# Running maximum over the feed-forward channels: halving of pieces replaced by a chain of joins, with new orders on all engines

## The chip, the cores and the metric

The kernel runs on 1 core of one Trainium2 chip. The metric is the time of one execution on the device in microseconds (us), and less is better. An execution under the hardware profiler gives the trace; its time and its span (first to last instruction) are told apart below.

## The reference

Sixteen images are cut into 36 patches each, projected to 256 channels, joined with a class token and 128 text tokens (165 tokens per sample), and sent through one transformer block: windowed attention, then a feed-forward part whose inputs and weights are rounded to a few levels.

```python
h = tok(x, W_lin, b_lin, class_token, position_embeddings)   # (16, 37, 256)
h = concatenate([h, txt], axis=1)                            # (16, 165, 256)
h = h + attn(layernorm(h))       # 16 heads, 4 KV heads, rotary, keys within 32 positions
h = h + ffn(layernorm(h))

def act_quant(x):
    scale = 127.0 / clip(max(abs(x), axis=-1, keepdims=True), 1e-05)
    return clip(round(x * scale), -128, 127) / scale

def ffn(x):
    h = einsum('bsd,hd->bsh', act_quant(x), weight_quant(w1))   # 256 -> 1024 channels
    h = depthwise_conv1d(h, conv_w, conv_b)                     # 3 taps along the tokens
    h = silu(h)
    return einsum('bsh,dh->bsd', act_quant(h), weight_quant(w2))
```

The part that the change rewrites is `max(abs(x), axis=-1)` of the second `act_quant`: for each token the largest magnitude over 1024 channels.

## The kernel before

**Tiling.** Two samples make a pair: 330 tokens, 3 token tiles (t) of 110. There are 8 pairs (n = 0 to 7). Attention goes over 11 blocks (j) of 30 queries with up to 94 keys. The feed-forward part has the 1024 channels in 8 tiles (m) of 128 partitions, each with 330 columns.

**The steps that the prediction names.** At the head: `sort_pix`, `turn_pix` and `keep_pix` reorder image rows, `patch` (L1636, L1638) projects a group of tokens, `keep_patch` copies it out, and SyncE's `move_tokens` moves it to `h` by DMA. `stats1_of` (L1337 to L1344) is the first layer norm's statistics; it waits for the tokens of its pair. `project` (L1689) makes queries, keys and values; `rope_first` (L1363 to L1378) or GpSimd's `rope` rotates them; `turn_q` (L1702) and `turn_k` (L1718) turn them; `keep_k_first` (L1384) copies keys out of PSUM. For each block `scores` (L1741 to L1752), `max_s` (L1393, VectorE), `shift` (L1760), `exp` (L1145), `turn_p` (L1769), `keep_p` (L1154) and `context` (L1784) follow one another. `abs_w` (L1307) sums the magnitudes of the feed-forward weights.

In the feed-forward part of a pair, `up` (L1840, L1841) fills a bank, ScalarE's `mid` (L1190) and VectorE's `taps` (L1449, L1452) do the convolution into `u`, `tanh` (L1198) with `silu` (L1458 on VectorE, L1043 and L1045 on GpSimd) gives the activation in place, and ScalarE's `abs_g` (L1206) writes magnitudes of a piece into the tile `ga`. A piece is 4 channel tiles (2 pieces a pair), and 2 channel tiles in the last pair (4 pieces).

**The maximum.** For pairs 0 to 6, `max_g` halves each piece: 4 tiles to 2 (L1475, 660 columns), 2 to 1 (L1479, 330 columns), and after the second piece joins the two results (L1482, 330 columns). In the last pair each piece of 2 tiles goes to 1 (L1468) and, from the second piece on, is joined to the result (L1473). The result is in `gm`. `turn_max` (L1849) turns it, `scale_2` (L1489 to L1495) makes the scale, `spread` (L1855) lays it over 128 partitions, `quant_g` (L1502) or `quant_last` (L1553) scales the activation to int8, `conv_g` (L1213) or `conv_last` (L1233) makes it bf16, `down` (L1867) multiplies, and `add_ffn` (L1510) adds to `h`. All pieces share `ga`, so `abs_g` of a piece waits (semaphore `part_maxed`) until the piece before it has been reduced.

**The last pair's input.** Its second layer norm goes tile by tile on VectorE: `var_last` (L1516, L1518), GpSimd's `rstd_last` (L1049), `norm_last` (seven instructions, L1523 to L1540), `turn_last` (L1874), ScalarE's `high_last` (L1227) and VectorE's `low_last` (L1546).

**What sets the order.** Every engine runs its own instructions in order. Each step has a place number per engine in the table `ORDER` (or `ONCE`), written out by hand; each engine walks the numbers upward and issues what is due. Semaphores alone tie the engines together. GpSimd and SyncE have such tables as well.

## Time and profile before

| | |
|---|---|
| median of 3 runs | 401.66 us (400.25 to 404.05) |
| the profiled execution | 399.73 us |
| its span | 397.9 us |
| mean granted TensorE clock | 0.956 |
| TensorE busy | 343.9 us (86%) |
| VectorE busy | 302.5 us (76%) |
| ScalarE busy | 259.2 us (65%) |
| GpSimd busy | 248.2 us (62%) |

PE is the matmul engine (TensorE), PEld its weight loads, DVE is VectorE, ACT is ScalarE, POOL is GpSimd and SP is SyncE. Busy time is an average over stages that are bound by different things, so it is read stage by stage. A matmul's record can overlap the next one's, because they are pipelined.

### The profile page before, as it was taken

How to read it: one execution, taken by the hardware profiler on the slowest of the kernel's cores; microseconds unless marked ns; L12 is line 12 of the kernel's file. 1: busy time of each engine (PE TensorE's matmuls, PEld its weight loads, DVE VectorE, ACT ScalarE, POOL GpSimd, SP SyncE). 2: the span in 40 equal slices, each digit the busy share in tenths (PEclk: the TensorE clock that was granted, in tenths of full speed). 3: DMA queues.
4: the chain of work that ended last, by engine and by line, in shares of the span. 5: the costliest groups of instructions: out<-in, count | busy, mean ns of one | idle time of the engine just before them, and what ended most of it. 6: DMA issues, size and time to landing. Idle time of an engine off the chain costs nothing.

```text
span 397.9 us, 8286 instructions
## 1 busy us (share of the span) xinstructions
PE 343.9 (86%) x2910; PEld 267.9 (67%) x2910; DVE 302.5 (76%) x643; ACT 259.2 (65%) x486; POOL 248.2 (62%) x244
## 2 busy tenths in 40 slices
PE   1579999999999989999999997989989989844564
PEld 1356666767787668867986796778857857634454
DVE  2164548744568889897889759998888899898984
ACT  3232554857767869867887767679777787534732
POOL 3407189299899994999489957991760563051510
PEclk9998999999999999999999999999999999995856
DMA  7772161000000100020001002000010210001001
GB/s 233 170 163 55 34 213 28 16 13 15 26 20 18 35 1 3 17 59 20 6 18 33 9 18 61 17 0 2 2 26 22 69 49 1 2 0 36 1 16 52
DMA packets 20250, 15.71 MB, mean 39 GB/s; under 512 B 11035, under 2 KB 19160, under 8 KB 20209
## 3 DMA queue, kind: packets, MB, share of 16 engines
q1 hardware_dynamic: 19314, 14.02, 13.7%
q10 hardware_dynamic: 895, 1.16, 1.1%
q8 instruction: 23, 0.38, 0.4%
q14 instruction: 18, 0.15, 0.1%
HBM read 7.91 MB, written 2.70 MB: 27 GB/s over the span
## 4 chain that ended last, share of the span: by engine, by line
PE 49%; DVE 20%; POOL 14%; issue 6%; DMA 5%; ACT 4%; SPq 1%; ACTq 0%; DVEq 0%; POOLq 0%
PE bank L1769 6%; PE bank L1840 4%; PE bank L1867 4%; PE bank L1784 3%; PE bank L1841 3%; POOL shared L1027 3%; PE bank L1741 3%; PE bank L1689 3%; PE bank L1760 3%; PE bank L1811 3%; DMA cst<-in_consts 3%; PE bank L1636 2%; POOL shared L1035 2%; PE bank L1752 2%; PE bank L1802 2%
## 5 line engine op out<-in xcount | busy, mean ns | idle before, releaser
L1393 DVE TENSOR_REDUCE mx<-bank 120x4 fp32r<-120x376 f32 (+3 forms) x88 | 44.5, 509 | 29.7 <-PE bank L1752 28.9
L1154 ACT COPY pT<-bank 94x480 f32<-94x480 f32 (+3 forms) x88 | 48.6, 555 | 15.4 <-PE bank L1769 14.9
L1145 ACT ACTIVATE pr<-bank 120x376 f32<-120x376 f32 (+3 forms) x88 | 39.9, 457 | 26.0 <-PE bank L1760 25.2
L1769 PE MATMUL bank<-cst,pr 120*94 120x120 f32 (+3 forms) x352 | 51.1, 269 | 3.2 <-ACT pr L1145 2.8
L1840 PE MATMUL bank<-xT_hi,w1T 128*128 128x330 f32 x128 | 45.6, 362 | 4.1 <-DVE wn L1452 2.4
L1769 PEld LDWEIGHTS bank<-cst,pr 120*94 120x94 f32 (+3 forms) x352 | 36.6, 121 | 12.5 <-ACT pr L1145 6.7
L1841 PE MATMUL bank<-xT_lo,w1T 128*128 128x330 f32 x128 | 41.1, 326 | 0.0
L1689 PE MATMUL bank<-wqk,xnT 128*110 128x384 f32 x96 | 36.8, 512 | 0.2
L1760 PE MATMUL bank<-mx,neg_id 120*120 120x376 f32 (+3 forms) x88 | 33.0, 386 | 4.0 <-DVE mx L1393 3.9
L1867 PE MATMUL bank<-w2T,shared 128*110 128x256 bf16 x192 | 29.2, 305 | 8.0 <-DVE h L1510 3.7
L1752 PE MATMUL bank<-kbd,q_hl 128*120 128x376 f32 (+3 forms) x88 | 36.1, 410 | 0.0
L1741 PE MATMUL bank<-kbd,q_hl 128*120 128x376 f32 (+3 forms) x88 | 35.6, 405 | 0.5 <-ACT pT L1154 0.4
L1043 POOL TENSOR_TENSOR shared<-shared,wn 128x1320 f32<-128x1320 f32 (+1 forms) x5 | 12.2, 2436 | 35.0 <-ACT shared L1198 35.0
L983 POOL TENSOR_SCALAR xn<-h,mv,rs 110x256 f32<-110x256 f32 x21 | 27.9, 1336 | 9.6 <-PE bank L1677 9.4
L1784 PE MATMUL bank<-pT,vw 94*32 94x120 f32 (+3 forms) x704 | 33.5, 286 | 0.2
L1867 PEld LDWEIGHTS bank<-w2T,shared 128*110 128x110 bf16 x192 | 24.6, 146 | 10.6 <-issue 5.3
L976 POOL TENSOR_TENSOR rs<-ve,half_neg 110x3 f32<-110x3 f32 x15 | 15.1, 1005 | 25.5 <-DVE ve L1344 18.9
L1027 POOL TENSOR_SCALAR shared<-h,mv,rs 110x256 f32<-110x256 f32 x21 | 30.2, 1449 | 1.1 <-POOL rs L976 1.1
L1840 PEld LDWEIGHTS bank<-xT_hi,w1T 128*128 128x128 f32 x128 | 25.5, 199 | 7.3 <-DVE wn L1452 3.2
L1035 POOL TENSOR_SCALAR shared<-shared,am 110x256 f32<-110x256 f32 x21 | 25.4, 1220 | 6.4 <-ACT shared L1174 6.4
L1005 POOL TENSOR_TENSOR qkr<-rc,rsn 110x160 f32<-110x160 f32 x44 | 26.8, 631 | 1.7
L1784 PEld LDWEIGHTS bank<-pT,vw 94*32 94x32 f32 (+3 forms) x704 | 18.8, 144 | 12.1 <-issue 8.2
(149 smaller groups left out, 918.4 us busy)
## 6 DMA issues: line engine op xcount, KB each, us to landing
out<-h SPq DMA_DIRECT2D x7, 330.0 KB
...
```

What stands on the lines that cost most here:

```text
L1027: o = nc.gpsimd.tensor_scalar(xn2[:, t, :], h[:, n, t, :], mv2[:, t, 0:1], rs2[:, t:t + 1], ALU.subtract, ALU.mult)
L1154: nc.scalar.copy(pT[0:cnt, g % 3, :], S_BANKS[g % 2][0:cnt, 0:HKV * QP]).then_inc(p_kept, 1)
L1393: nc.vector.tensor_reduce(mx[:, g % 4, :].bitcast(F32R), S_BANKS[g % 2][0:QP, 0:HKV * KEYS[j][1]].rearrange("p (k c) -> p k c", k=HKV), ax ...
L1689: o = nc.tensor.matmul(qk_bank(n, t)[0:TT, 0:QKC + QK], xnT[:, k, t * TT:(t + 1) * TT], wqk[:, k, :], start=(k == 0), stop=(k == KD - 1))
L1741: nc.tensor.matmul(dst, q, kbd[n % 2][:, 0, :, k0:k0 + cnt].bitcast(F32R), start=True, stop=False)
L1752: o = nc.tensor.matmul(dst, q, kbd[n % 2][:, 1, :, k0:k0 + cnt].bitcast(F32R), start=False, stop=True)
L1760: nc.tensor.matmul(S_BANKS[g % 2][0:QP, 0:HKV * cnt], neg_id[:, :].bitcast(F32R), mx[:, g % 4, :].bitcast(F32R).unsqueeze(2).to_broadcast( ...
L1769: o = nc.tensor.transpose(S_BANKS[g % 2][0:cnt, kv * QP:(kv + 1) * QP], pr[:, g % 3, kv * cnt:(kv + 1) * cnt], ident[0:QP, 0:QP])
L1784: o = nc.tensor.matmul(C_BANK[VS * kv:VS * (kv + 1), col:col + QP], vw[n % 2][0:cnt, j, :, kv], pT[0:cnt, g % 3, kv * QP:(kv + 1) * QP], s ...
L1840: nc.tensor.matmul(dst, w, xT_hi[:, k, :].bitcast(F32R), start=(k == 0), stop=False)
L1841: o = nc.tensor.matmul(dst, w, xT_lo[:, k, :].bitcast(F32R), start=False, stop=(k == KD - 1))
L1867: o = nc.tensor.matmul(down_bank(n, t), gq[:, m, t * TT:(t + 1) * TT], w2T[:, m, :], start=(m == 0), stop=(m == MH - 1))
```

## The change

The tile `ga` has 6 channel tiles in place of 4, and `gm` one in place of 3. In pairs 0 to 6 the first piece's magnitudes go to tiles 0 to 3 and the second's to tiles 2 to 5. Tiles 0 and 1 hold the running maximum and take in two more tiles at a time: one join of 660 columns for the first piece, two for the second, and at the end tile 0 with tile 1 into `gm` (330 columns). In the last pair the four pieces go to tiles 0, 2, 4 and 2, with three joins and the same end. Lines of the changed kernel are some 5 to 9 higher: the joins are L1482 there and the end is L1487.

```diff
+def ga_of(n, p):
+    if n < PAIRS - 1:
+        return (slice(0, 4), slice(2, 6))[p]
+    at = (0, 2, 4, 2)[p]
+    return slice(at, at + 2)
...
-        gm, at = carve(shared, at, 128, [3, T])
+        gm, at = carve(shared, at, 128, [T])
...
-        ga, at = carve(shared, at, 128, [HALFC, T])
+        ga, at = carve(shared, at, 128, [6, T])
...
             def abs_g(n, p):
-                at = NP * n + p
-                act.wait_ge(silued, at + 1)
-                if at:
-                    act.wait_ge(part_maxed, at)
                 ms = gate(n, p)
-                nc.scalar.activation(ga[:, 0:ms.stop - ms.start, :], u_of(n)[:, ms, :], ACT.Abs).then_inc(g_absed, 1)
+                act.wait_ge(silued, NP * n + p + 1)
+                if n and p == 0:
+                    act.wait_ge(g_maxed, n)
+                if p and ga_of(n, p).start == 2 and (n < PAIRS - 1 or p > 1):
+                    act.wait_ge(joined, 3 * n + 1)
+                nc.scalar.activation(ga[:, ga_of(n, p), :], u_of(n)[:, ms, :], ACT.Abs).then_inc(g_absed, 1)
...
             def max_g(n, p):
...
+                    joins = ((), (2,), (4,), (2,))[p]
+                    first = 3 * n + p
+                else:
+                    joins = ((2,), (2, 4))[p]
+                    first = 3 * n + p + 1
+                if joins:
+                    dve.wait_ge(g_absed, NP * n + p + 1)
+                for i, at in enumerate(joins):
+                    if first + i > 3 * n + 1:
+                        dve.wait_ge(joined, first + i - 1)
+                    nc.vector.tensor_tensor(ga[:, 0:2, :], ga[:, 0:2, :], ga[:, at:at + 2, :], ALU.max).then_inc(joined, 1)
+                if gate(n, p).stop == MH:
+                    dve.wait_ge(joined, 3 * (n + 1))
+                    if n:
                         dve.wait_ge(max_turned, n)
...
+                    nc.vector.tensor_tensor(gm[:, :], ga[:, 0, :], ga[:, 1, :], ALU.max).then_inc(g_maxed, 1)
...
             def turn_max(n):
-                pe.wait_ge(g_maxed, n + (1 if n < PAIRS - 1 else 3))
+                pe.wait_ge(g_maxed, n + 1)
```

Nearly all rows of `ORDER` and `ONCE` change too, on all engines. Two of them:

```diff
-    'pe.patches': (1, 9, 10, 16),
+    'pe.patches': (1, 8, 11, 12),
...
-    'dve.norm_last': (284, 293, 300),
+    'dve.norm_last': (281, 298, 299),
```

**TensorE at the head**, from the first `turn_q` (L1702 before, L1707 now) to the first `scores` (L1741 before, L1746 now). L1636 and L1638 (now L1641 and L1643) are `patch`, L1718 (now L1723) is `turn_k`. Before:

```order
L1689 MATMUL bank<-wqk,xnT 110x384 x6
L1636 MATMUL bank<-wlT,wn 126x256 x6
L1638 MATMUL bank<-posb,cst 126x256
L1636 MATMUL bank<-wlT,wn 126x256 x6
L1638 MATMUL bank<-posb,cst 126x256
L1702 MATMUL bank<-cst,qsp 128x110 x8
L1718 MATMUL bank<-cst,qsp 128x110 x6
L1702 MATMUL bank<-cst,qsp 128x110 x4
L1636 MATMUL bank<-wlT,wn 126x256 x6
L1638 MATMUL bank<-posb,cst 126x256
L1741 MATMUL bank<-kbd,q_hl 120x264
```

Now:

```order
L1694 MATMUL bank<-wqk,xnT 110x384 x2
L1707 MATMUL bank<-cst,qsp 128x110 x4
L1641 MATMUL bank<-wlT,wn 126x256 x6
L1643 MATMUL bank<-posb,cst 126x256
L1641 MATMUL bank<-wlT,wn 126x256 x6
L1643 MATMUL bank<-posb,cst 126x256
L1707 MATMUL bank<-cst,qsp 128x110 x4
L1723 MATMUL bank<-cst,qsp 128x110 x6
L1707 MATMUL bank<-cst,qsp 128x110 x4
L1682 MATMUL bank<-cst,xn 128x110 x3
L1746 MATMUL bank<-kbd,q_hl 120x264
```

The last `patch` stood between `turn_k` and the first `scores`; now it stands ahead of `turn_k`, and 3 transposes of the next pair's `xn` stand in its place.

**VectorE at the head**, from the copy of the first pair's keys (L1384 before, L1393 now) on. L1337 to L1344 (now L1346 to L1353) are `stats1_of`, L1393 (now L1402) is `max_s`, L1307 (now L1316) is `abs_w`. Before:

```order
L1384 TENSOR_SCALAR kbd<-bank,cst 128x330 x4
L1393 TENSOR_REDUCE mx<-bank 120x4 x2
L1337 BN_STATS st<-h 110x6 x3
L1341 BN_AGGR mv<-st 110x2 x3
L1344 TENSOR_SCALAR ve<-mv 110x3
L1393 TENSOR_REDUCE mx<-bank 120x4 x4
L1307 TENSOR_REDUCE wabs<-wn 128x1
L1393 TENSOR_REDUCE mx<-bank 120x4
```

Now:

```order
L1393 TENSOR_SCALAR kbd<-bank,cst 128x330 x4
L1346 BN_STATS st<-h 110x6 x3
L1350 BN_AGGR mv<-st 110x2 x3
L1353 TENSOR_SCALAR ve<-mv 110x3
L1402 TENSOR_REDUCE mx<-bank 120x4 x2
L1346 BN_STATS st<-h 110x6 x3
L1350 BN_AGGR mv<-st 110x2 x3
L1353 TENSOR_SCALAR ve<-mv 110x3
L1402 TENSOR_REDUCE mx<-bank 120x4 x2
L1316 TENSOR_REDUCE wabs<-wn 128x1 x2
L1402 TENSOR_REDUCE mx<-bank 120x4 x2
```

The statistics of pair 2 stood behind the first two maxima and now stand ahead of them; the two sums over weights stand together, ahead of the fifth maximum.

**VectorE at the end of pair 6**, around the last pair's input. L1523 (now L1528) begins `norm_last` and L1540 (now L1545) ends it, L1458 of 1320 columns (now L1467) is `silu`, L1475 to L1482 (now L1482 and L1487) are `max_g`, L1546 (now L1551) is `low_last`. Before:

```order
L1523 TENSOR_SCALAR shared<-h,mv,rs 110x256
...
L1540 TENSOR_SCALAR shared<-shared,am 110x256
L1449 SCALAR_TENSOR_TENSOR shared<-bank,conv,shared 128x2x164
...
L1458 SCALAR_TENSOR_TENSOR shared<-shared 128x1320
L1523 TENSOR_SCALAR shared<-h,mv,rs 110x256
...
L1475 TENSOR_TENSOR shared<-shared 128x660
L1479 TENSOR_TENSOR shared<-shared 128x330
L1546 TENSOR_TENSOR xT_lo<-bank,xT_hi 128x2x220
```

Now:

```order
L1461 SCALAR_TENSOR_TENSOR shared<-bank,conv,shared 128x2x164
L1521 BN_AGGR mv<-st 110x2
L1523 TENSOR_SCALAR ve<-mv 110x1
L1528 TENSOR_SCALAR shared<-h,mv,rs 110x256
...
L1545 TENSOR_SCALAR shared<-shared,am 110x256
L1528 TENSOR_SCALAR shared<-h,mv,rs 110x256
...
L1482 TENSOR_TENSOR shared<-shared 128x660
L1467 SCALAR_TENSOR_TENSOR shared<-shared 128x1320
L1551 TENSOR_TENSOR xT_lo<-bank,xT_hi 128x2x220
```

`norm_last` of tile 1 stood with two channel tiles of `taps` behind it; now both `norm_last` steps stand together behind all `taps` of the pair, and `silu` stands behind them.

## Rows read from the trace of the kernel before

**Rows 1.** Busy time by stretch, each engine in turn, granted clock, DMA share, GB/s

```profile
40.00:60.00 20.00, 19.06 (x131) 13.42 (x131) 10.40 (x24) 10.91 (x25) 10.54 (x14) 1.00 0.37 123
...
80.00:100.00 20.00, 19.65 (x184) 14.53 (x183) 9.04 (x27) 12.71 (x26) 19.09 (x24) 1.00 0.06 14
...
160.00:180.00 20.00, 19.26 (x170) 14.53 (x169) 18.89 (x42) 14.87 (x29) 19.38 (x16) 1.00 0.15 38
...
360.00:380.00 20.00, 11.65 (x48) 9.88 (x48) 18.49 (x38) 11.62 (x16) 6.36 (x4) 0.67 0.02 8
```

**Rows 2.** The chain that ended last, shares of the span by engine

```profile
PE 49%; DVE 20%; POOL 14%; issue 6%; DMA 5%; ACT 4%; SPq 1%; ACTq 0%; DVEq 0%; POOLq 0%
```

**Rows 3.** TensorE in order of time, 27 to 48 us

```profile
27.64 0.94 PE L1623 MATMUL bank<-cst,shared 72*128 72x72 f32 x12 [0.16 <-DVE wn L1298]
...
40.74 0.98 PE L1702 MATMUL bank<-cst,qsp 110*128 110x110 f32 x8
41.91 0.76 PE L1718 MATMUL bank<-cst,qsp 110*128 110x110 f32 x6 [0.19 <-DVE qsp L1378]
...
42.87 2.77 PE L1636 MATMUL bank<-wlT,wn 128*126 128x256 f32 x12
...
46.20 0.39 PE L1741 MATMUL bank<-kbd,q_hl 128*120 128x264 f32 x1
...
47.35 0.37 PE L1760 MATMUL bank<-mx,neg_id 120*120 120x264 f32 x1
```

**Rows 4.** VectorE in order of time, 42 to 58 us

```profile
42.70 1.97 DVE L1384 TENSOR_SCALAR kbd<-bank,cst 128x330 fp32r<-128x330 f32 x4 [0.94 <-PE bank L1718]
...
46.87 1.00 DVE L1393 TENSOR_REDUCE mx<-bank 120x4 fp32r<-120x264 f32 x2 [2.20 <-PE bank L1752]
...
49.20 1.08 DVE L1337 BATCH_NORM_STATS2 st<-h 110x6 f32<-110x256 f32 x3 [1.33 <-DMA h<-tokp]
...
50.66 0.17 DVE L1344 TENSOR_SCALAR ve<-mv 110x3 f32<-110x3 f32 x1
...
57.81 2.28 DVE L1307 TENSOR_REDUCE wabs<-wn 128x1 f32<-128x2048 f32 x1
```

**Rows 5.** SyncE's queue in order of time, 31 to 48 us

```profile
31.53 13.09 SPq L922 DMA_DIRECT2D vw<-qk  x17
44.66 3.03 SPq L900 DMA_DIRECT2D h<-tokp  x4
```

**Rows 6.** VectorE by line: instructions of the maximum, busy us and mean ns

```profile
L1475 DVE TENSOR_TENSOR shared<-shared 128x660 f32<-128x660 f32 x14 | 13.3, 952 | 1.1 <-ACT shared L1206 0.8
...
L1479 DVE TENSOR_TENSOR shared<-shared 128x330 f32<-128x330 f32 x14 | 10.9, 777 | 0.5
...
L1482 DVE TENSOR_TENSOR shared<-shared 128x330 f32<-128x330 f32 x7 | 4.9, 699 | 0.2
```

**Rows 7.** The wide ones: duration in ns min/median/max

```profile
L1475 DVE TENSOR_TENSOR shared<-shared x14: 836/848/1577, 133.4 to 364.8; 128x660 f32<-128x660 f32 x14
```

**Rows 8.** VectorE in order of time, 342 to 360 us

```profile
342.81 0.35 DVE L1537 TENSOR_SCALAR shared<-shared,am 110x256 f32<-110x256 f32 x1
...
345.51 0.56 DVE L1452 SCALAR_TENSOR_TENSOR shared<-bank,conv,shared 128x328 f32<-128x328 f32 x1
...
349.89 1.16 DVE L1523 TENSOR_SCALAR shared<-h,mv,rs 110x256 f32<-110x256 f32 x1
...
352.04 2.05 DVE L1537 TENSOR_SCALAR shared<-shared,am 110x256 f32<-110x256 f32 x1
...
359.95 0.41 DVE L1523 TENSOR_SCALAR shared<-h,mv,rs 110x256 f32<-110x256 f32 x1 [0.44 <-POOL rs L1049]
```

**Rows 9.** GpSimd in order of time, 347 to 354 us

```profile
347.88 3.02 POOL L1043 TENSOR_TENSOR shared<-shared 128x1320 f32<-128x1320 f32 x1
350.97 2.97 POOL L1045 TENSOR_TENSOR shared<-shared 128x1320 f32<-128x1320 f32 x1
```

**Rows 10.** VectorE in order of time, at 384 us

```profile
384.56 0.50 DVE L1468 TENSOR_TENSOR shared<-shared 128x330 f32<-128x330 f32 x1 [0.34 <-ACT shared L1206]
```

More of the change, by code:

```diff
@@ L147 @@
+        (24, 28, 39),
+        (86, 90, 96),
+        (136, 141, 144),
+        (191, 195, 202),
+        (253, 264, 277),
+        (338, 343, 348),
+        (405, 415, 420),
     ),
     'pe.turn_q': (
-        (11, 12, 15),
-        (46, 57, 66),
-        (105, 116, 121),
-        (154, 169, 174),
-        (208, 225, 230),
-        (287, 300, 312),
-        (360, 371, 384),
-        (447, 452, 460),
+        (10, 13, 16),
+        (43, 47, 57),
+        (101, 113, 121),
+        (153, 169, 172),
@@ L157 @@
+        (206, 224, 232),
+        (289, 298, 318),
+        (352, 367, 385),
+        (438, 453, 460),
     ),
     'pe.turn_k': (
-        (13, 14),
-        (68, 73),
-        (124, None),
-        (179, None),
-        (239, None),
-        (322, None),
-        (387, None),
-        (485, None),
+        (14, 15),
+        (64, 71),
+        (125, None),
+        (176, None),
+        (237, None),
+        (324, None),
+        (393, None),
+        (495, None),
     ),
     'pe.scores': (
[8 rows of a table removed]
[8 rows of a table added]
@@ L262 @@
-        (533, 542, 554),
-        (581, 592, 601),
+        (234, 242, 257),
+        (304, 314, 332),
+        (382, 398, 425),
+        (470, 482, 490),
+        (528, 536, 561),
+        (590, 596, 599),
         (616, 617, 618),
@@ L333 @@
-        (283, 305, 318),
-        (340, 352, 366),
-        (384, 402, 414),
+        (31, 46, 58),
+        (75, 92, 104),
+        (125, 146, 162),
+        (189, 198, 217),
+        (237, 253, 264),
+        (284, 303, 322),
+        (340, 352, 369),
+        (385, 398, 412),
     ),
     'act.keep_sel': (
-        (39, 51, 64),
-        (83, 97, 111),
-        (135, 154, 169),
-        (193, 205, 226),
+        (39, 51, 65),
+        (84, 101, 113),
+        (138, 155, 171),
+        (195, 206, 226),
@@ L447 @@
         (31, None),
-        (40, None),
+        (39, None),
         (50, None),
```

369 lines of the change are left out of this document (167 added, 202 removed), and 160 rows, old and new, of the table ORDER.

## The prediction

> **What bounds the kernel now.** I read the table of busy time by stretch first, since whole-span shares mix stages [rows 1]. The reader is to see three regimes. Up to about 150 us TensorE is nearly always busy (19.65 of 20 us at 80 to 100 us) and GpSimd too (19.09), while VectorE has half its time free (9.04). From 160 us on VectorE is nearly as full as TensorE (18.89 and 19.26). After 360 us VectorE alone is full (18.49) and TensorE is at 11.65. The chain of work that ended last says the same: TensorE 49%, VectorE 20%, GpSimd 14% [rows 2]. So time taken from VectorE is worth nothing early, something in the middle, and all of it at the end; and a delay of TensorE at the head is not easily won back.
>
> The profiled execution took 399.73 us with a span of 397.9; the median of the runs is 401.66, that is 1.93 above it. I make the sum as a difference to the profiled execution and put it on the median.
>
> **The joins.** Per pair (0 to 6) before: two instructions of 660 columns and three of 330. After: three of 660 and one of 330. The columns are equal (2310); one instruction fewer is issued and two narrow ones become one wide. By the means of the trace before [rows 6]: 2 x 0.952 + 2 x 0.777 + 0.699 = 4.157 us; after: 3 x 0.952 + 0.699 = 3.555 us; 0.60 less. By the shortest wide one [rows 7] and a narrow one of 0.50 [rows 10]: 2 x 0.836 + 3 x 0.50 = 3.17 and 3 x 0.836 + 0.50 = 3.01; 0.16 less. The two differ because narrow instructions ran much longer than 0.50 us on average (0.777, 0.699), and wide ones up to 1.577: each seems to pay for something on top of its columns, so fewer instructions pay less often. I take 0.4 a pair, between the two. It counts where VectorE is last to come: pairs 2 to 6, five pairs, 2.0 us. Pairs 0 and 1 fall before or about 160 us, where VectorE has room. Bounds: 5 x 0.16 = 0.8 and 7 x 0.60 = 4.2. Term: **-2.0** (0.8 to 4.2 less). The new waits (`joined`) stand on instructions that were in a chain before too, and the second piece's magnitudes now wait for one instruction, not two.
>
> There is a rule that speaks against wide joins. The long ones have a partner: a VectorE instruction of 0.35 us took 2.05 us while GpSimd ran one of 2.97, and it ended 0.15 us behind that one's end (352.04 + 2.05 = 354.09, and 350.97 + 2.97 = 353.94) [rows 8, 9]. The Trainium skill, "SBUF — State Buffer" (the part on the port pair that VectorE and GpSimd share), says that the pair is an exclusive lock held for a whole instruction, and counts a VectorE instruction with two SBUF inputs among those that contend. By that rule GpSimd in turn waits for a join up to 0.85 us where it waited up to 0.50, and pair 0's three joins lie in GpSimd's full stretch: 3 x 0.35 = 1.05 us later there, and the whole sum would be -1.7 where it is -2.7 without. The trace bears out the lock, but shows no GpSimd instruction that waits for a join alone, so I leave it out of the sum and inside the range.
>
> **The head.** Two moves work together, and both go against the kernel. First, TensorE. Before, `turn_k` began at 41.91, the copy of the keys ran from 42.70 to 44.67 while the last `patch` ran (42.87 to 46.20), and `scores` began at 46.20 with no wait [rows 3, 4]. Now that `patch` stands ahead of `turn_k`. What comes before it is otherwise the same work, less the turns that move behind (one of the two `turn_q` that began at 40.74, and all up to 42.87: about 1.6 us) and plus one `turn_pix` (0.94 us) that began at 27.64, when the engine had idle time, and now stands behind the first `project`; the patches end near 46.20 - 1.6 + 0.95 = 45.5, `turn_k` begins near 46.0, the key copy starts 0.8 later and ends near 48.8. `scores` start there, 2.6 us later, and only a short transpose fills the gap. Second, VectorE. `stats1_of` of pair 2 now stands ahead of the first `max_s`. It waits for tokens that landed at 49.20, and they cannot come sooner: SyncE issues them at 44.66 to 47.69, behind 17 transfers that it issues from 31.53 without a break [rows 4, 5], and SyncE's order up to there is unchanged. The statistics end at 50.66 + 0.17 = 50.83, and the first `max_s` starts there and not at 46.87: **4.0 us later**. `shift` follows it as before (47.35). In that time TensorE does about 0.5 us of work that came later before, so it is 3.5 us behind.
>
> How much of that is still there at the end? TensorE in 40 to 60 us was busy 19.06 of 20 [rows 1], so there is 0.9 us per 20 to win back, about 1.3 up to 80 us by this and a little more by the weights, whose second sum now stands beside the first and not apart. I take **+2.2**. Bounds: 0 (all of it hidden later) and +3.9, and with the two sums over weights together ahead of the fifth `max_s` (2.28 us more in one piece [rows 4]) up to +6.2.
>
> **The end of pair 6.** Before, `norm_last` of tile 1 met GpSimd's `silu`. Its first instruction took 1.16 us and its sixth 2.05, where the first took 0.41 for tile 2 and the sixth 0.35 for tile 0 [rows 8]; each ended just after a GpSimd instruction of 3 us ended (350.90 and 353.94) [rows 9]. That is 0.75 + 1.70 = 2.45 us, on an engine that is full there, and 0.44 us of idle time before tile 2's step comes on top: 2.9. In the new order `norm_last` of tiles 1 and 2 stand behind all eight `taps`. GpSimd's `silu` started 1.8 us after the fourth channel tile's taps ended (346.07 to 347.88) and lasted 6.1, till +7.9; VectorE has about 7.3 us of other work up to `norm_last` (four more channel tiles at 2 x 0.56, two `add_ffn`, one attention add with its statistics, one normalization of the context). So it gets there near the end of `silu`, and one small instruction (`ve`, 0.17 us) may wait up to 0.8. Term: -2.9 + 0.8 = **-2.1**, bounds 0 (another instruction waits in place of these) and -2.9. What is late next: `low_last` then follows `silu` on VectorE, which covers the way over TensorE and ScalarE.
>
> **The last pair.** Four instructions (3 x 0.85 + 0.50 = 3.05) for seven (7 x 0.50 = 3.5) [rows 7, 10]: 0.45 less, on the path, since VectorE is full here. The idle gap of 0.34 ahead of the last piece [rows 10] should close: `tanh` of the first piece stands earlier, and the last piece's magnitudes go to other tiles than the piece before and need no longer wait for it. Against it: behind the last magnitudes there are now 0.85 + 0.50 us and not 0.50 + 0.50. Term: **-0.8**, bounds 0 and -1.1. From `gm` to the end nothing changes.
>
> **The middle.** All rows move by a few places. The number of matmuls is the same, and counting what stands ahead of each pair's steps gives shifts of either sign of about 1 us. I cost it at 0, with 2.5 us to either side from the size of one such stall in the rows (2.05) [rows 8].
>
> **The sum.** -2.0 + 2.2 - 2.1 - 0.8 + 0 = -2.7 us. The profiled execution would be 397.0 us, the median 401.66 - 2.7 = **399.0 us**.
>
> **Rivals.**
> 1. *The head decides.* First `max_s` 4 us late, then the two weight sums in one piece hold `max_s` back again: +6.2, against gains of 2.0 + 2.1 + 0.8 = 4.9. That gives +1.3, 403.0 us, slower than before. It decides from a head loss of 4.9 us on. For it speaks that TensorE and GpSimd have under 1 us of slack in 20 at 80 to 100 us; against it that VectorE has half its time free there, so that what comes late to it does not queue as well.
> 2. *VectorE's relief counts everywhere.* Joins at the mean, all seven pairs (-4.2), head mostly hidden (+0.5), the end as forecast (-2.1 - 0.8): -6.6, 395.1 us. For it: VectorE's 18.89 of 20 at 160 us; against: TensorE's 19.26 there [rows 1].
> 3. *The end's waits only move.* The lock takes as much in another place (0 for the end of pair 6), joins hidden (-0.8), head +1.5, last pair -0.5: +0.2, 401.9 us. For it: contention goes by chance of place, and the new order was not the only thing that kept these apart. This is also the case in which the change of the maximum does not do what it says.
>
> **Chances.** Forecast (397.5 to 401) 0.39; rival 1 and what lies above 402.5 0.16; rival 2 and what lies below 397.5 0.28; rival 3 0.17. The range reaches from rival 2 to a little past rival 1, so that about 0.1 is left out at either end: 395.0 to 403.8. About 1% (4 us) is what a measurement of this kernel can tell from no change. Faster by over 1% means under 397.6: rival 2's 0.28 and the lowest 0.03 of the forecast, 0.31. Slower by over 1% means over 405.7, which is rival 1 with the middle's 2.5 us against it as well (405.5) and beyond: 0.10. Between: 0.59.
>
> **What would show it.** Head: VectorE's first TENSOR_REDUCE of `mx` near 50.8 and first `scores` near 48.8; if the maximum comes near 47, the head step is wrong. Statistics of pair 2 waiting for the DMA till 49.2 just ahead of it. TensorE's busy time in 40 to 60 us falls by some 2 us. Joins of pairs 0 to 6: the wide ones near 0.95 on average, and with the last narrow ones some 25 us in sum, not 13.3 + 10.9 + 4.9 = 29.1 [rows 6]. End of pair 6: both `norm_last` steps about 2.1 us each with no instruction over 1 us. Last pair: no idle time ahead of its last joins. The prediction fails if the middle moves by more than 2.5 us: then one of the new places puts a step of VectorE or GpSimd behind a wait that nobody needs.

## The result

The changed kernel is slower: the median of four runs is 407.12 us (405.46 to 409.70), of the kernel before beside it 402.86 us, ratio 1.014 with a 95% interval of 1.008 to 1.020. Medians are over all runs, while every ratio here and below leaves out runs in the chip's slower state, among them one of 407.82 us of the kernel before, whose other three have the median of 401.66 that the prediction started from. The forecast was 399.0 us, 2.7 less than 401.66; measured are 5.5 more. The profiled execution took 405.46 us with a span of 403.4, against 399.73 and 397.9. The table by stretch, columns as in [rows 1]:

```profile
40.00:60.00 20.00, 16.68 (x89) 11.07 (x87) 10.89 (x29) 7.67 (x19) 10.27 (x13) 0.83 0.38 127
80.00:100.00 20.00, 19.75 (x179) 14.97 (x176) 10.33 (x28) 15.02 (x30) 15.64 (x21) 1.00 0.05 11
160.00:180.00 20.00, 18.34 (x153) 14.11 (x150) 17.01 (x34) 15.48 (x29) 17.02 (x10) 1.00 0.15 37
360.00:380.00 20.00, 10.03 (x40) 8.15 (x39) 18.33 (x41) 11.01 (x15) 6.29 (x4) 0.64 0.02 6
```

From 40 to 60 us TensorE is busy 16.68 us in place of 19.06, issues 89 instructions in place of 131, and its granted clock is 0.83 and no longer 1.00. The chain that ended last, by engine (against [rows 2]), has more TensorE, less VectorE, and SyncE's queue in it:

```profile
PE 65%; DVE 10%; SPq 7%; ACT 6%; issue 4%; POOL 4%; DMA 3%; ACTq 0%; DVEq 0%; POOLq 0%
```

TensorE in order of time, 44 to 58 us, where [rows 3] went from the turn of the keys through the last patch into the scores:

```profile
44.08 0.73 PE L1723 MATMUL bank<-cst,qsp 110*128 110x110 f32 x6
...
47.04 0.47 PE L1682 MATMUL bank<-cst,xn 110*128 110x110 f32 x3 [1.85 <-ACT q_hl L1131]
47.37 0.36 PE L1746 MATMUL bank<-kbd,q_hl 128*120 128x264 f32 x1
...
50.23 1.11 PE L1765 MATMUL bank<-mx,neg_id 120*120 120x264 f32 x2 [0.80 <-DVE mx L1402]
...
52.09 2.77 PE L1694 MATMUL bank<-wqk,xnT 128*110 128x384 f32 x4
...
55.25 0.41 PE L1746 MATMUL bank<-kbd,q_hl 128*120 128x376 f32 x1
```

VectorE in order of time, 44 to 62 us (against [rows 4]):

```profile
44.84 1.97 DVE L1393 TENSOR_SCALAR kbd<-bank,cst 128x330 fp32r<-128x330 f32 x4 [3.33 <-PE bank L1723]
48.21 1.08 DVE L1346 BATCH_NORM_STATS2 st<-h 110x6 f32<-110x256 f32 x3 [1.40 <-DMA h<-tokp]
...
49.75 0.87 DVE L1402 TENSOR_REDUCE mx<-bank 120x4 fp32r<-120x264 f32 x2
54.76 1.08 DVE L1346 BATCH_NORM_STATS2 st<-h 110x6 f32<-110x256 f32 x3 [4.13 <-POOL xn L991]
...
57.34 4.47 DVE L1316 TENSOR_REDUCE wabs<-wn 128x1 f32<-128x2048 f32 x2
```

The first `scores` began at 47.37 and not 46.20, the first `max_s` at 49.75 and not 46.87, both with a wait ahead of them: TensorE's 1.85 us are for ScalarE's copy of the turned queries (L1131), VectorE's 1.40 us for the tokens of pair 2. A second wait of 4.13 us stands on the statistics of pair 3, which are held by GpSimd's norm of pair 2. The projection of four matmuls at 52.09 took 2.77 us, at half the clock (1.54 us before). The granted clock (last but two column) in steps of 4 us, 46 to 58 us:

```profile
46.00:50.00 4.00, 2.33 (x12) 1.64 (x12) 2.53 (x10) 1.65 (x5) 0.07 (x1) 0.79 0.48 144
50.00:54.00 4.00, 3.77 (x9) 2.23 (x10) 0.63 (x2) 1.92 (x5) 3.82 (x4) 0.50 1.02 377
54.00:58.00 4.00, 3.81 (x17) 2.44 (x16) 3.13 (x10) 1.03 (x2) 3.09 (x5) 0.85 0.22 66
```

0.50 is the 1.2 GHz level. The clock fell between 48 and 49 us, behind the wait of 1.85 us and ahead of the one of 0.80. Against full speed the 12 us lack 4 x (0.21 + 0.50 + 0.15) = 3.4 us of clock, idle time included.

I followed one mark through both traces: the start of TensorE's `turn_xn` of pair n. Pair 2's came 3.6 us later than before (76.9), pair 3's 4.0 (101.5), pair 5's 3.8 (163.0), pair 6's 4.7 (204.5), and the run ended 5.5 later. Pair 1's scores came 3.3 us later (81.49 and 78.15). So about 4 of the 5.5 us are lost by pair 3's mark, and nothing wins them back. In between it is more for a time: pair 7's mark is 6.8 us late. The maximum itself did what it should; VectorE by line (against [rows 6]):

```profile
L1482 DVE TENSOR_TENSOR shared<-shared 128x660 f32<-128x660 f32 x24 | 22.3, 931 | 0.9 <-ACT shared L1215 0.6
L1487 DVE TENSOR_TENSOR shared<-shared 128x330 f32<-128x330 f32 x8 | 4.8, 604 | 0.3
```

The last pair's four are in it (0.84 + 0.84 + 0.85 + 0.51 = 3.04 us from 386 to 391 us), so those of pairs 0 to 6 take 27.1 - 3.0 = 24.1 us in place of 29.1. At the end of pair 6 `norm_last` of tile 1 runs from 362.40 to 364.55 without a long instruction, for GpSimd's `silu` was over by then (to 362.43):

```profile
362.40 0.41 DVE L1528 TENSOR_SCALAR shared<-h,mv,rs 110x256 f32<-110x256 f32 x1
...
363.81 0.35 DVE L1542 TENSOR_SCALAR shared<-shared,am 110x256 f32<-110x256 f32 x1
```

### The profile page after: what moved, and what is told of

Its sections match the earlier page's. It is cut to its first block, busy times and chain, and to the rows that moved or that the text cites. A ratio compares the mean times of both kernels' runs of the same rounds, so it can differ in the third digit from the quotient of the medians.

```text
span 403.4 us, 8281 instructions
## 1 busy us (share of the span) xinstructions
PE 351.0 (87%) x2910; PEld 272.4 (68%) x2910; DVE 295.3 (73%) x633; ACT 260.7 (65%) x486; POOL 244.8 (61%) x244
## 4 chain that ended last, share of the span: by engine, by line
PE 65%; DVE 10%; SPq 7%; ACT 6%; issue 4%; POOL 4%; DMA 3%; ACTq 0%; DVEq 0%; POOLq 0%
PE bank L1774 8%; PE bank L1694 7%; PE bank L1789 6%; SPq L930 6%; PE bank L1816 5%; PE bank L1845 5%; PE bank L1872 4%; PE bank L1746 4%; PE bank L1846 4%; PE bank L1765 4%; PE bank L1807 3%; PE bank L1757 3%; PE bank L1641 2%; DMA cst<-in_consts 2%; DVE shared L1482 2%
## 5 line engine op out<-in xcount | busy, mean ns | idle before, releaser
L1402 DVE TENSOR_REDUCE mx<-bank 120x4 fp32r<-120x376 f32 (+3 forms) x88 | 44.7, 511 | 35.5 <-PE bank L1757 35.0
L1845 PE MATMUL bank<-xT_hi,w1T 128*128 128x330 f32 x128 | 46.6, 368 | 5.5 <-DVE wn L1461 2.8
L1846 PE MATMUL bank<-xT_lo,w1T 128*128 128x330 f32 x128 | 42.3, 335 | 0.0
L1746 PE MATMUL bank<-kbd,q_hl 128*120 128x376 f32 (+3 forms) x88 | 35.9, 408 | 4.1 <-ACT pT L1162 3.8
L1765 PE MATMUL bank<-mx,neg_id 120*120 120x376 f32 (+3 forms) x88 | 35.7, 409 | 2.4 <-DVE mx L1402 1.9
L991 POOL TENSOR_SCALAR xn<-h,mv,rs 110x256 f32<-110x256 f32 x21 | 26.0, 1248 | 12.9 <-PE bank L1682 12.5
L1845 PEld LDWEIGHTS bank<-xT_hi,w1T 128*128 128x128 f32 x128 | 26.3, 206 | 8.7 <-DVE wn L1461 4.0
L1035 POOL TENSOR_SCALAR shared<-h,mv,rs 110x256 f32<-110x256 f32 x21 | 29.3, 1404 | 1.2 <-POOL rs L984 1.1
L1872 PEld LDWEIGHTS bank<-w2T,shared 128*110 128x110 bf16 x192 | 25.5, 149 | 5.3 <-ACT shared L1242 2.5
L1013 POOL TENSOR_TENSOR qkr<-rc,rsn 110x160 f32<-110x160 f32 x44 | 27.8, 654 | 1.7
L1198 ACT ACTIVATE shared<-bank,conv 128x330 f32<-128x330 f32 x32 | 20.0, 627 | 12.6 <-PE bank L1846 11.7
```

The lines of the kernel that those rows point to most:

```text
L1402: nc.vector.tensor_reduce(mx[:, g % 4, :].bitcast(F32R), S_BANKS[g % 2][0:QP, 0:HKV * KEYS[j][1]].rearrange("p (k c) -> p k c", k=HKV), ax ...
L1746: nc.tensor.matmul(dst, q, kbd[n % 2][:, 0, :, k0:k0 + cnt].bitcast(F32R), start=True, stop=False)
L1765: nc.tensor.matmul(S_BANKS[g % 2][0:QP, 0:HKV * cnt], neg_id[:, :].bitcast(F32R), mx[:, g % 4, :].bitcast(F32R).unsqueeze(2).to_broadcast( ...
L1845: nc.tensor.matmul(dst, w, xT_hi[:, k, :].bitcast(F32R), start=(k == 0), stop=False)
L1846: o = nc.tensor.matmul(dst, w, xT_lo[:, k, :].bitcast(F32R), start=False, stop=(k == KD - 1))
L1872: o = nc.tensor.matmul(down_bank(n, t), gq[:, m, t * TT:(t + 1) * TT], w2T[:, m, :], start=(m == 0), stop=(m == MH - 1))
```

## The experiments

Each kernel was timed in five rounds beside the kernel before, and those of a group on the same chip (`e18` and `e19` on another than the rest of their group). In the tables of places a number is only a rank, so an edit is shown as the move that it makes.

**First group: which part?** The places up to the start of the third pair ("the head") and the rest were crossed.

`e1`: the chain in the code, all old places.

> The chain of joins in the code, all tables of places of the kernel before (piece 0 of the last pair has no join and so no item). Theory T1 (the new order at the head costs about 4 us, the chain itself is worth little): 401.4 to 402.4 where the kernel before shows 402.9, a ratio of 0.996 to 1.000, first max_s(0,0) within 0.5 us of the kernel before. Rival R1 (the chain itself makes the loss: its joins wait on the abs, abs on the join): 405 or more, ratio over 1.005. Rival R2 (the joins are worth the full 2 us of the forecast and only the new order hid it): 400.9 or less, ratio under 0.995.

402.64 us, ratio 0.998 (0.993 to 1.003). As T1 had it. The lower end of the interval is 2.7 us under the kernel before, so it leaves room for R2's 2 us as well.

`e2`: the halving in the code, all new places.

> The halving of pieces as in the kernel before, with the new tables of places (the last pair's piece 0 gets its place back, behind its last taps). T1: the loss of the head is all there, 406.5 to 408.5, ratio 1.009 to 1.014. R1: the loss goes with the chain, 402 to 404, ratio under 1.004. R2: slower than the changed kernel by 2 us, 409, ratio 1.015.

408.55 us, ratio 1.012 (1.006 to 1.019). The loss is there without the chain: R1 is refuted.

`e3` and `e4`: the chain with old head and new rest, and with new head and old rest.

> The chain, and on each engine the items of the old order up to the start of the third pair (TensorE's first 77 items, VectorE's 33, ScalarE's 55, GpSimd's 11, SyncE's 8), then all others in the new order. T1: the 3.5 to 4 us that the traces show by 78 us are gone, 402.4 to 404.0, ratio 0.999 to 1.003. Rival R3 (the middle of the new order loses as much by itself, and would lose it with any head): 406 or more, ratio over 1.008.

> The mirror of the kernel with the old head: the chain, the items of the new order up to the start of the third pair, then all others in the old order. T1: 405.5 to 407, ratio 1.007 to 1.011. R3: 402.5 to 403.5, ratio under 1.003.

401.61 us, 0.998 (0.995 to 1.001), and 408.82 us, 1.015 (1.009 to 1.022). The order at the head is the whole loss: 1.8% or 7 us from `e1` to `e4`, by the intervals some 4 to 10. The new order behind it costs nothing that can be measured. In the trace of `e4` the second pair's scores start 4.5 us later than before, and the mark of pair 3 does too. In `e3` the same stretch has the full clock:

```profile
46.00:50.00 4.00, 3.63 (x24) 2.63 (x22) 0.97 (x2) 1.04 (x3) 0.00 (x0) 1.00 0.15 38
50.00:54.00 4.00, 3.73 (x26) 2.27 (x23) 2.11 (x8) 2.22 (x6) 2.05 (x3) 1.00 0.93 286
```

**Second group: which move of the head, and what is a join worth?** My theory was that the two statistics on VectorE make the loss.

```diff
 dve, e5: changed kernel with
-  stats1(2), max_s(0,0), max_s(0,1), stats1(3), max_s(0,2) ...
+  max_s(0,0), max_s(0,1), stats1(2), max_s(0,2) ... max_s(0,6), stats1(3)
 pool, e5:
-  rope(1,0), rstd1(3), rope(1,1), rope(1,2)
+  rope(1,0), rope(1,1), rope(1,2), rstd1(3)
```

> The changed kernel with the statistics of pair 2 behind max_s(0,1) and those of pair 3 behind max_s(0,6) again, and GpSimd's rstd1 of pair 3 behind rope(1,2), as before; all else new. Theory T1s (the loss at the head is made by the two waits of the statistics on VectorE, for a transfer and for GpSimd's norm, and by the TensorE clock that falls behind them): first max_s near 48, clock 1.00 from 48 to 58, start of the second pair's scores 2.5 to 4 us earlier than in the changed kernel, time 403 to 404.5. Rival T1p (the loss comes from TensorE's own gap of 1.85 us at 45 to 47, where the last patches no longer fill the wait for ScalarE, and the clock falls for that): the clock still falls to 0.5, at least 2 us of the loss stay, 406 or more.

407.86 us, 1.012 (1.007 to 1.016). The clock stays at 1.00 from 46 to 62 us as T1s says, and yet nothing is won. TensorE in order of time, near 67 us:

```profile
62.21 1.33 PE L1907 MATMUL bank<-cst,pr 120*78 120x120 f32 x8
66.83 0.74 PE L1840 MATMUL bank<-cst,qsp 110*128 110x110 f32 x4 [3.30 <-POOL qsp L1160]
```

This is `turn_q(1,1)`, which waits for GpSimd's rope of pair 1. The new order has it ahead of `scores(0,6)`, the old one behind `scores(0,8)`. Behind the wait the clock is 0.65 from 66 to 70 us. Both theories fall: one stall is gone and another has its place.

`e6` puts only the statistics of pair 3 back.

> The changed kernel with only the statistics of pair 3 (and GpSimd's rstd1 of pair 3) back at their old places; those of pair 2 stay ahead of max_s(0,0). If the second wait of 4.1 us on VectorE costs what its place suggests: 404.5 to 405.5, start of the second pair's scores 1.5 to 2.5 us earlier than in the changed kernel. If TensorE at half its clock reaches the third scores only at 55.3 anyway, so that the wait is covered: 406.5 to 407.5, under 0.7 us earlier.

404.95 us, 1.003 (0.999 to 1.008); in the trace, whose execution was the longest of its six (406.82), the wait of 4.1 us is gone and pair 3's mark is at 105.7 us against 105.5 in the changed kernel. The trace is for "covered", the median for the other; I leave it open. The interval lies wholly below that of the changed kernel (1.008 to 1.020), though that was timed in another session, so this one move may hold a good part of the loss.

```diff
 pe, e7: changed kernel with
-  patches 2, patches 3, turn_q(0,1), turn_k(0,0), turn_k(0,1), turn_q(0,2)
+  patches 2, turn_q(0,1), turn_k(0,0), turn_k(0,1), turn_q(0,2), patches 3
```

> The changed kernel with the last patches of TensorE (patches 3) behind turn_q(0,2) again, in the gap of 1.85 us ahead of the second pair's turn_xn; all else new, both statistics ahead as in the change. T1s: TensorE still waits for the first max_s, the clock still falls, 406 to 408. T1p: the gap is filled, the clock stays at 1.00 from 46 to 56, start of the second pair's scores 2 to 3 us earlier, 404 to 405.

405.63 us, 1.006 (1.001 to 1.010), profiled 406.96. The gap of 1.85 us is filled, the first scores start 1.5 us earlier, and TensorE waits for the first maximum instead, with the clock at 0.51 from 50 to 54 us again:

```profile
47.13 0.42 PE L1890 MATMUL bank<-kbd,q_hl 128*120 128x368 f32 x1
50.71 1.11 PE L1898 MATMUL bank<-mx,neg_id 120*120 120x264 f32 x2 [3.15 <-DVE mx L1535]
```

`e10`, on `e1`, does each join twice in pairs 0 to 6:

```diff
+                    if n < PAIRS - 1:
+                        nc.vector.tensor_tensor(ga[:, 0:2, :], ga[:, 0:2, :], ga[:, at:at + 2, :], ALU.max).then_inc(rejoined, 1)
+                        dve.wait_ge(rejoined, first + i)
                     nc.vector.tensor_tensor(ga[:, 0:2, :], ga[:, 0:2, :], ga[:, at:at + 2, :], ALU.max).then_inc(joined, 1)
```

> The chain with the old tables of places, and in pairs 0 to 6 each join of two tiles is done twice (the maximum is not changed by it): 21 more instructions of about 0.93 us, 19.5 us more of VectorE's busy time, 2.8 us per pair. Theory T2 (in the middle TensorE's queue sets the end and the joins lie beside it): 402.5 to 405, so under 2 us for 19.5. Rival (half of the joins' time shows, which is how the prediction came to 2.0 us for 4.1): 412 or more.

428.37 us, 1.063 (1.059 to 1.067). T2 falls: 21 more joins of 0.998 us on average (20.9 us) cost 25.4 us, more than they last. (The rival ascribes to the prediction that half of the joins' time shows; it had counted 0.4 us in each of five pairs in full.) The marks tell where: against the kernel before, pair 4's is 0.3 us late, when no join has run yet, pair 5's 4.0, pair 6's 8.3 and pair 7's 11.5.

**Third group: up and down from the joins, and two more moves.** `e12` cuts the joins of pairs 0 to 6 to 8 columns a tile (`ga[:, 0:2, 0:8]`), `e13` repeats only the last join of a pair.

> The chain with the old tables of places; in pairs 0 to 6 each join of two tiles takes the maximum of 8 columns of each tile alone (the others are left out, so most tokens get a scale from 2 tiles only), 21 instructions of about 0.1 us for 0.93: 17 us less of VectorE's busy time. Theory T4 (what is saved on VectorE is not wanted there: TensorE's queue is 94 to 99 per cent busy in the middle): 401 to 402.5, less than 2 us. Rival (VectorE sets the pace in the middle, as the kernel with each join done twice has it, 25 us for 19.5): 396 or less.

399.82 us, 0.993 (0.990 to 0.996), so 2.9 us less. That lies between the two, nearer to T4. It does not decide R2, since it measures from the chain downwards and not from the halving to the chain. The 21 short joins took 0.31 us each and not 0.1. VectorE by line has all 24 joins at 9.1 us, where `e1` has 23.4:

```profile
L1616 DVE TENSOR_TENSOR shared<-shared 128x16 f32<-128x16 f32 (+1 forms) x24 | 9.1, 379 | 1.6 <-ACT shared L1348 1.0
```

> The chain with the old tables of places, and in pairs 0 to 6 only the last join of a pair is done twice: 7 more instructions of 0.93 us, 6.5 us more of VectorE's time, 0.9 per pair. In proportion to the kernel with 21 more, 25.7 us for 19.5, it would be 411; if there is slack below a step of that size, 403 to 406.

419.21 us, 1.041 (1.036 to 1.047): 16.7 us for 7 instructions of 1.162 us. The trace has a wait of 2.4 us for `qsp` and the clock at 0.65 from 46 to 50 us before there is any join, and its first scores come at 49.88, 3.7 us later than before. Counted from the first scores to the end it is 14.7 us longer than `e1`'s trace. Downwards 14.3 us of joins bring 2.9; upwards 8.1 us cost 15 to 17. TensorE in order of time at 150 us shows how:

```profile
147.83 0.60 PE L1843 MATMUL bank<-cst,qsp 110*128 110x110 f32 x4
150.34 0.54 PE L1990 MATMUL bank<-cst,shared 128*110 128x128 f32 x3 [1.91 <-DVE shared L1623]
...
151.17 0.95 PE L1910 MATMUL bank<-cst,pr 120*94 120x120 f32 x4
```

and by stretch, same kernel:

```profile
145.00:150.00 5.00, 2.96 (x23) 1.65 (x21) 4.77 (x6) 3.23 (x7) 4.92 (x6) 1.00 0.00 0
150.00:155.00 5.00, 4.66 (x25) 4.54 (x26) 3.28 (x11) 1.03 (x2) 4.75 (x7) 0.66 0.00 0
```

`turn_max` stands in TensorE's queue where the maximum has just come; 1.91 us late, TensorE idles, and then works at a lower clock (four transposes 0.95 us, where they took 0.57 at full clock). Against the kernel before, pair 2's scores come 3.8 us late and pair 3's 6.2: 2.4 us for one join more.

`e9` undoes one swap: GpSimd's `norm1(2)` behind `rope(1,0)`.

> The changed kernel with one swap undone: GpSimd's norm1 of pair 2 behind rope(1,0) again instead of ahead of it. The statistics of pair 3 on VectorE still wait for that norm. If the wait on VectorE is what costs (the prediction's way of thinking), it grows from 4.1 us by the rope's 3 to 4 us and all later maxima with it: second pair's scores at 84 or later, 409 or more. If the late rope costs instead (it hands TensorE the second pair's turned queries), the time falls: second pair's scores 1 to 2 us earlier than in the changed kernel, 405 to 406.

416.13 us, 1.032 (1.027 to 1.037). The prediction's way of thinking holds here. VectorE, then TensorE, in order of time:

```profile
64.35 1.08 DVE L1479 BATCH_NORM_STATS2 st<-h 110x6 f32<-110x256 f32 x3 [13.20 <-POOL xn L1124]
...
66.49 1.12 PE L1898 MATMUL bank<-mx,neg_id 120*120 120x376 f32 x2 [7.58 <-DVE mx L1535]
```

`e11` takes back the statistics and GpSimd's order at once.

> The changed kernel with both statistics on VectorE at their old places (as in the kernel with both back, where TensorE then waited 3.3 us for GpSimd's rope of pair 1 and its clock fell there), and GpSimd's first eleven items in the old order. Theory T3 (the three moves belong together: statistics early so that the norm can stand ahead of the rope; it takes both undone to be rid of the loss): no wait for the rope near 63 to 67, clock 1.00 from 48 to 75, second pair's scores at 78 to 80, 402.5 to 404. Rival T1p2 (the rest of the new order at the head, TensorE's and ScalarE's, costs by itself): 406 or more.

408.91 us, 1.017 (1.011 to 1.022). The wait for the rope is still 3.24 us, the clock 0.64 behind it: T3 falls: what is left of the new head costs by itself. That is TensorE's and ScalarE's places, as the rival says, but also VectorE's for the weights, which `e11` keeps.

**Fourth group: TensorE's turn.**

```diff
 pe, e14 (on e11) and e15 (on the changed kernel):
-  turn_q(1,1), scores(0,6), scores(0,7) ... turn_q(1,2), scores(0,8)
+  scores(0,6), scores(0,7) ... scores(0,8), turn_q(1,1), turn_q(1,2)
 act: keep_q(1,1) behind exp(0,7)
 pe, e16 (on e1):
-  turn_q(1,0), context(0,4), shift(0,6) ... scores(0,8), turn_q(1,1)
+  turn_q(1,0), turn_q(1,1), context(0,4), shift(0,6) ... scores(0,8)
 act: keep_q(1,1) right behind keep_q(1,0)
```

> The chain with the old tables and one move of the new order alone: TensorE's turn_q(1,1) right behind turn_q(1,0) instead of behind scores(0,8), ScalarE's keep_q(1,1) right behind keep_q(1,0). T5: TensorE waits for GpSimd's rope till about 65, 3 to 4 us, its clock falls to 0.5 behind that, the second pair's scores are 3 to 5 us later than with the old tables alone, 406 to 408. Rival: the queues have slack there, 402.6 as with the old tables, under 1 us more.

410.34 us, 1.019 (1.015 to 1.023), against 0.998 for the same kernel without the move. TensorE in order of time, then its stretch behind that row:

```profile
65.89 1.00 PE L1840 MATMUL bank<-cst,qsp 110*128 110x110 f32 x4 [2.36 <-POOL qsp L1160]
```

```profile
66.00:70.00 4.00, 4.00 (x38) 2.57 (x39) 0.00 (x0) 1.32 (x3) 3.75 (x7) 0.50 0.14 34
```

TensorE waits 2.36 us, runs the next 4 us at 1.2 GHz, and pair 1's scores come 5.1 us later than in `e1`, counted from the first scores. One such move alone costs as much as the whole change. It is not quite the changed kernel's: there `turn_q(1,1)` stands ahead of `scores(0,6)`, here behind it and ahead of `scores(0,7)`.

> The changed kernel with only turn_q(1,1) and (1,2) on TensorE and keep_q(1,1) on ScalarE moved back, as in the kernel above; statistics and GpSimd as changed. T5: the first maxima are late and the clock falls as in the changed kernel, but scores 6 to 8 of pair 0 no longer wait for the rope: second pair's scores 1 to 2 us earlier than in the changed kernel, 405 to 406. Rival (the wait for the statistics sets everything behind it): no gain, 407.

406.63 us, 1.012 (1.008 to 1.015). Pair 3's mark is at 104.6 us against 105.5, but TensorE's first `turn_xn` is as much earlier (26.14 against 27.02), ahead of anything that was moved. Counted from the first scores the mark gains 0.1 us, and the time is not clear of the changed kernel's: the rival holds.

> The kernel with both statistics and GpSimd's order back (408.9 us, a wait of 3.2 us of TensorE for the rope), and besides TensorE's turn_q(1,1) and (1,2) behind scores(0,8) instead of ahead of scores(0,6) and (0,8), with ScalarE's keep_q(1,1) behind exp(0,7). Theory T5 (three moves make the loss: statistics, norm and turn; the early place of turn_q(1,1) is what a late rope hits): the wait falls below 1 us, clock 1.00 from 46 to 78, second pair's scores at 78 to 80, 403 to 404.5. Rival: what is left of the new order on TensorE and ScalarE costs by itself, 406 or more.

407.60 us, 1.017 (1.013 to 1.022). `turn_q(1,1)` starts at 69.66 without a wait, and the next one is caught:

```profile
69.66 0.54 PE L1840 MATMUL bank<-cst,qsp 110*128 110x110 f32 x4
73.84 0.59 PE L1840 MATMUL bank<-cst,qsp 110*128 110x110 f32 x4 [3.65 <-POOL qsp L1160]
```

It is `turn_q(1,2)`, which I had put right behind it, while in the old order it comes later; GpSimd's third rope ended at 73.79, against 69.39 before. GpSimd in order of time shows one step of the rope at twice its length (0.86 before):

```profile
62.30 1.85 POOL L1141 TENSOR_TENSOR rsn<-qk,cst 110x320 f32<-110x320 f32 x1
```

On VectorE the rounding of the first weights runs beside it (`L1464`, 1.44 us from 61.99). So T5 is right that an early turn can cost (`e16`), and wrong that three moves make up the loss. Two more kernels followed that.

```diff
 pe, e18 (on e14):
-  turn_q(1,1), turn_q(1,2) ... turn_k(1,0) ... shift(0,9)
+  turn_q(1,1) ... shift(0,9), turn_q(1,2), turn_k(1,0)
 act: keep_q(1,2), keep_k(1,0) behind exp(0,9)
 e19 (on e18): dve, first 33 items in the old order;
 pe: sum_w behind shift(0,8), turn_w(0) behind select(0,1)
```

> The kernel with statistics, GpSimd's order and turn_q(1,1) back, and besides turn_q(1,2) and turn_k(1,0) behind shift(0,9) on TensorE, keep_q(1,2) and keep_k(1,0) behind exp(0,9) on ScalarE, about where they stood before. Theory T6 (each early turn is a meeting with GpSimd's rope; with none of them early, what is left is the late start and the weights): no wait of TensorE over 1.5 us between 50 and 78 us, clock 1.00 there, start of turn_xn of pair 3 at 103 to 104.5 us, 403.5 to 405.5. Rival T7 (some further place of the new order catches the wait again): a wait of 2 us or more before 80 us, 406 or more.

406.83 us, 1.011 (1.006 to 1.016). No wait for the rope is left, and ScalarE's copy of the keys is the next to catch TensorE, ahead of the second half of the keys' turn:

```profile
75.17 0.50 PE L1856 MATMUL bank<-cst,qsp 110*128 110x110 f32 x3 [0.62 <-ACT q_hl L1264]
77.57 0.74 PE L1856 MATMUL bank<-cst,qsp 110*128 110x110 f32 x3 [1.78 <-ACT kbd L1270]
```

> The same, and besides VectorE's first 33 items wholly in the old order (the sums over the weights and their rounding apart and later), TensorE's sum_w behind shift(0,8) and turn_w(0) behind select(0,1). T6: GpSimd's steps of the rope no longer meet the rounding (none over 1.2 us between 60 and 70 us), turn_xn of pair 3 at 102.5 to 103.5 us, 402.5 to 404, about 1 us less than the kernel with the second turn back. Rival T7: 406 or more, as all others with a part of the new head.

409.67 us, 1.017 (1.013 to 1.022). GpSimd's steps are back at 0.86 and its third rope ends at 70.93 (73.79 in `e14`), so the weights were what stretched it. But now the three roundings of the first weights stand ahead of the second pair's first maximum, and TensorE waits for that. VectorE, then TensorE:

```profile
76.12 1.22 DVE L1468 TENSOR_SCALAR wn<-wn 128x2048 f32<-128x2048 f32 x1
77.37 1.23 DVE L1472 TENSOR_SCALAR w1q<-wn 128x2048 bf16<-128x2048 f32 x1
78.51 0.42 DVE L1535 TENSOR_REDUCE mx<-bank 120x4 fp32r<-120x264 f32 x1
```

```profile
78.99 0.57 PE L1898 MATMUL bank<-mx,neg_id 120*120 120x264 f32 x1 [3.16 <-DVE mx L1535]
```

T7's times hold in both kernels. Its wait of 2 us or more is there in `e19`; in `e18` it is 1.78 us, which still breaks T6's 1.5, and the clock is at 0.61 from 78 to 82 us behind it.

> The chain with the old order up to the last pair's context (TensorE's first 547 items, VectorE's 262, ScalarE's 381, GpSimd's 56, SyncE's 24), then the new order. The prediction's terms for the end (2.1 us at the end of pair 6 and 0.8 in the last pair) would give 399.7 against 402.6 for the old tables alone, ratio 0.991. If TensorE's clock and the chain behind the last down take that back: 401 to 402.5, ratio 0.996 or more.

402.95 us, 1.002 (0.999 to 1.005), no gain over `e1` (0.993 to 1.003). In the traces the last pair's `turn_ctx` is 3.6 us behind the kernel before, its `up` 2.2, its `turn_max` 1.7, and the span 2.4; in `e1` these are 2.4, 2.2, 2.2 and 2.6.

Start of `turn_xn` of pair 3 in the traces (us), the same counted from the first scores, and the longest wait of TensorE between 44 and 80 us:

| kernel | pair 3 | from the first scores | longest wait, for |
|---|---|---|---|
| before | 101.5 | 55.3 | 0.6, ScalarE's exp |
| old places (e1) | 102.6 | 55.3 | 0.6, the same |
| old head (e3) | 102.2 | 55.0 | 0.6, the same |
| changed | 105.5 | 58.2 | 1.85, ScalarE's copy of the queries |
| new head (e4) | 106.1 | 59.7 | 1.85, the same |
| e5 | 106.6 | 58.7 | 3.30, GpSimd's rope |
| e6 | 105.7 | 57.8 | 1.85, ScalarE's copy |
| e7 | 106.2 | 60.4 | 3.15, VectorE's maximum |
| e9 | 116.0 | 68.1 | 7.58, VectorE's maximum |
| e11 | 106.6 | 58.6 | 3.24, GpSimd's rope |
| e14 | 107.7 | 59.4 | 3.65, GpSimd's rope |
| e15 | 104.6 | 58.0 | 1.85, ScalarE's copy |
| e16 | 108.1 | 60.5 | 2.36, GpSimd's rope |
| e18 | 106.4 | 58.2 | 1.85, ScalarE's copy |
| e19 | 109.6 | 61.2 | 3.16, VectorE's maximum |

The first scores start from 0.4 us earlier to 2.1 us later than before in these runs, so differences under 1 us in the first column say little. The second says more: `e10`, `e12`, `e13` and `e17`, whose order up to there is the old one, have 55.3 too, and every kernel with the new head or a part of it has at least 57.8. The wait of 1.85 us stands ahead of the first scores and is not in that column.

## Why the prediction was wrong

**The head** is the step that failed: "+2.2, bounds 0 and +3.9". Measured are 4.0 us in the changed kernel's trace and 4.5 in `e4`'s, both at pair 3's mark, 7 us of time from `e1` to `e4`, and 1.1 to 1.7% of the time in nine kernels that have the new head or most of it (0.3 and 0.6% in `e6` and `e7`, 3.2 in `e9`). Its direction was right, and its first stall had the place and the cause that the prediction gave: the statistics wait for the transfer. The first `max_s` came 2.9 us late, not 4.0, since the tokens were there at 48.2 and not 49.2: with the first projection ahead of a `turn_pix`, SyncE's 17 transfers began at 30.54 and not at 31.53, which the prediction had held impossible. TensorE's side came out otherwise. `turn_k` began at 44.08 and not near 46.0, so the copy of the keys (over by 46.8) did not set the first scores. TensorE waited for the copy of the queries instead, and the scores came at 47.37 and not 48.8. Some 1.2 of the 1.9 us at `turn_k` are the clock's: the twelve projections took 5.76 us in the trace before and 1.51 + 1.49 + 1.54 = 4.54 in this one. By stretch, before and changed:

```profile
28.00:34.00 6.00, 6.00 (x22) 3.34 (x20) 0.92 (x3) 0.96 (x3) 2.41 (x4) 0.72 0.59 123
28.00:34.00 6.00, 5.58 (x30) 4.14 (x31) 1.87 (x5) 2.91 (x9) 3.31 (x6) 1.00 0.65 145
```

The prediction's rows held a stretch at the lower clock that is not tied to the order: in `e1`, with the old order, the clock is at 1.00 there. Three things more were not in it.

First, TensorE's clock. The prediction took idle time of TensorE at its own length. In the changed kernel 3.4 us of clock are missing between 46 and 58 us, and in `e16` 2.36 us of waiting cost 5.1. The clock alone is not the loss: in `e5` and `e11` it stays at 1.00 there and falls only near 67 us, and the loss is as large. Second, it counted only VectorE's and one of TensorE's moves. The second wait (statistics of pair 3, 4.13 us) and `turn_q(1,1)` ahead of `scores(0,6)` are in the diff's table and were not followed. Third, it let the loss be won back from idle time ("0.9 us per 20"). It was not: the mark is 3.6 us late at pair 2 and 3.8 at pair 5.

**Rival 1**, "the head decides", had the right place and nearly the size: its +6.2 lies in what `e4` against `e1` leaves open. Its mechanism does not show. The fifth maximum did come behind both sums (61.73), but TensorE waited for no maximum between 56 and 68 us, and nowhere there for more than 0.41. Moving the sums alone was not tried.

**The joins**, "-2.0 (0.8 to 4.2 less)", are mis-sized in what VectorE's time is worth. The check of 25 us for pairs 0 to 6 was met (24.1), and by itself the chain saves 0.4 us a pair (26.3 us in `e1` for 29.1), as the prediction had it. In time `e1` brought 0.8 us (2.7 less to 1.0 more). `e12` took away another 14.3 us and brought 2.9, 0.2 for 1; if that rate held for the first 5.0 us too, which no run shows, they would bring 1.0 (an estimate). So "five pairs" in full was probably too much, and is not excluded; **rival 2**, which had 4.2 us in seven pairs, is refuted by `e1`, and so is its contrary that the joins lie beside the path, by `e10` and `e13`.

**The end of pair 6** and **the last pair**: as mechanisms they came as forecast, two steps of 2.1 us, no idle time ahead of the last joins. "-2.1" and "-0.8" did not show in the time: `e17` would have had to be at 0.991 and is at 1.002 (0.999 to 1.005). `e1` has the same long instructions as before (1.14 and 2.06 us) and `e17` has not (none over 0.42), and the last pair's `up` starts equally late in both. From there to the last `turn_max` `e17` gains 0.5 us, and at the end of the span 0.2 of it is left. The prediction named `low_last` as covering what comes next; that the time stays the same is measured, which step holds it was not tried.

Together: the head lies 4 to 5 us above its term, the two end terms of 2.9 us are missing, and the joins perhaps 1 short. That makes up the 8.1 us between the forecast and the result, as far as such parts can be added.

**The middle**, "0, with 2.5 to either side": right as far as the time shows. `e3` against `e1` shows no difference, and the stretch from 101.5 to 163.0 us before took 61.3 us after. Between the marks of pairs 5 and 7 the changed kernel and `e3` both lose 3.0 us against the kernel before (75.9 for 72.9), and `e3`'s time has none of it; where it comes back was not followed.

**Still open**: how the loss of the head divides. `e5`, `e7`, `e11`, `e14`, `e15`, `e18` and `e19` each took a stall away, and each time another took its place at nearly the same price: rope at `turn_q(1,1)`, first maximum, rope at `turn_q(1,2)`, copy of the keys, maximum of the next pair. `e6` may be the exception, by its time. Shown is that one early turn alone is enough for the loss (`e16`), that it isn't needed for it (`e15`, `e18`), and that the old head as a whole is rid of it (`e3`). All seven kept the new start, with its 1.85 us of waiting or, in `e7`, 3.15 in its place; the new start alone with the old order behind it was not tried.
